# A fused four-layer network on one core: other orders and semaphores in the router stage, the layer-0 feed-forward and the 16-head attention

## The reference

```python
x = x + tanh(g_xattn[0]) * L0_xattn(layernorm(x), ctx, ...)      # attention, one head
x = x + tanh(g_ffn[0])   * L0_ffn(layernorm(x), W_up, W_down, W_gate, W_expert)
x = x + tanh(g_xattn[1]) * L1_xattn(...)                         # 32 heads, rotary
x = x + tanh(g_ffn[1])   * L1_ffn(...)                           # ternary weights
x = x + tanh(g_xattn[2]) * L2_xattn(layernorm(x), ctx, Wq, Wk, Wv, Wo, gq, gk)
x = x + tanh(g_ffn[2])   * L2_ffn(layernorm(x), w_router, wg, wu, wd, ...)
x = x + tanh(g_xattn[3]) * L3_xattn(ctx, layernorm(x), ...)      # scan over 16 states
x = x + tanh(g_ffn[3])   * L3_ffn(layernorm(x), weight)          # fp8 blocks

# L2_xattn: 16 heads of 128; q and k are divided by their root mean square
q = rmsnorm(hidden @ Wq, gq); k = rmsnorm(ctx @ Wk, gk); v = ctx @ Wv
out = softmax(q @ k.T / sqrt(128)) @ v @ Wo

# L2_ffn: 8 routed experts, 2 for each token, beside a shared expert with a gate
probs = softmax(x @ w_router.T); top_v, top_i = top_k(probs, 2)
out = sum over the two of top_v * (silu(x @ wg.T) * (x @ wu.T)) @ wd.T
out += sigmoid(x @ gate_w.T) * (silu(x @ sw_gate.T) * (x @ sw_up.T)) @ sw_down.T
```

## Time and profile before

| what | value |
|---|---|
| runs | 3429.04, 3439.06, 3434.04 us, median 3434.04 |
| profiled execution | 3425.45 us, its span 3423.7 us |
| PE, DVE, ACT, POOL busy | 3077.1, 2608.9, 1870.1, 1471.5 us (90, 76, 55, 43%) |
| layer-0 feed-forward | about 212 to 404 us of the span |
| 16-head attention | about 1400 to 2712 us |
| router stage | about 2712 to 2869 us |

### The profile page before, as it was taken

How to read it: one execution, slowest core, us unless ns; L and a number is a source line. 1 busy time by engine, 2 the same in 40 slices (tenths; PEclk the granted TensorE clock), 3 DMA queues, 4 the chain that set the end, 5 groups by cost and what they waited for, 6 DMA issues and landing times. The chain is left out here.

```text
span 3423.7 us, 43286 instructions
## 1 busy us (share of the span) xinstructions
PE 3077.1 (90%) x14500; PEld 1876.2 (55%) x14500; DVE 2608.9 (76%) x3454; ACT 1870.1 (55%) x3464; POOL 1471.5 (43%) x965
## 2 busy tenths in 40 slices
PE   7969788999997999699999999999998697998985
PEld 3447554333334556465656556655655376786663
DVE  7955688877774999288888888888888764766886
ACT  5654343666664677466666566666666333663220
POOL 1132378000000010177777777778877653224430
PEclk9989999999998999899999999999999898999998
DMA  4147645222214222355565565555554356674321
GB/s 136 50 168 277 231 127 132 67 57 61 60 31 140 74 80 72 141 169 178 194 197 182 169 205 188 182 183 189 179 173 157 106 204 216 248 259 174 141 74 62
DMA packets 228071, 508.06 MB, mean 148 GB/s; under 512 B 36607, under 2 KB 70015, under 8 KB 209936
## 3 DMA queue, kind: packets, MB, share of 16 engines
q1 hardware_dynamic: 221616, 488.55, 43.2%
q0 software_dynamic: 6240, 16.81, 1.4%
HBM read 408.48 MB, written 100.45 MB: 149 GB/s over the span
## 5 line engine op out<-in xcount | busy, mean ns | idle before, releaser
L2473 POOL TENSOR_TENSOR l2x_inflow<-l2x_dtu,l2x_rows_b 128x512 f32<-128x512 f32 x256 | 438.5, 1713 | 217.4 <-DVE l2x_state L2359 211.0
L2489 POOL TENSOR_TENSOR l2x_y_sum<-l2x_y_sum,l2x_state 128x512 f32<-128x512 f32 x224 | 387.2, 1729 | 29.2 <-DVE l2x_state L2368 29.2
L2359 DVE TENSOR_TENSOR_SCAN l2x_state<-l2x_decay,l2x_inflow 128x512 f32<-128x512 f32 x256 | 391.8, 1530 | 0.3 <-issue 0.3
L1358 DVE TENSOR_REDUCE l1x_mx<-psum 128x2 f32<-128x1024 f32 x256 | 308.2, 1218 | 94.0 <-PE psum L1200 92.3
L1315 ACT ACTIVATE l1x_split<-psum 128x1024 f32<-128x1024 f32 x256 | 262.1, 1025 | 154.9 <-PE psum L1200 154.9
L186 POOL TENSOR_TENSOR ln_work<-ln_work,minus_half 128x4 f32<-128x4 f32 (+1 forms) x34 | 36.4, 1071 | 720.0 <-DVE ln_work L170 719.9
L2368 DVE TENSOR_TENSOR l2x_state<-l2x_state,l2x_rows_c 128x512 f32<-128x512 f32 x256 | 315.1, 1231 | 6.6
L2230 ACT ACTIVATE l2x_decay<-l2x_dt,a_neg 128x512 f32<-128x512 f32 x256 | 181.4, 721 | 194.2 <-DVE l2x_state L2359 194.2
L126 PE MATMUL psum<-l2x_probs_t,l2x_v_tok 128*128 128x512 f32 x512 | 234.9, 602 | 13.1 <-ACT l2x_qt L220 10.9
L2166 ACT ACTIVATE l2x_probs<-psum,l2x_soft,l2x_norms 128x512 f32<-128x512 f32 x256 | 195.9, 775 | 87.6 <-DVE l2x_soft L2297 87.6
L126 PE MATMUL psum<-l2x_kt,l2x_qt 128*128 128x512 f32 x512 | 228.7, 593 | 0.9 <-DVE x_res L226 0.9
(11 more groups left out here) (459 smaller groups left out, 7241.6 us busy)
## 6 DMA issues: line engine op xcount, KB each, us to landing
l2x_rows_b<-l3x_xd_dram SPq DMA_DIRECT2D x256, 256.0 KB, 3.9
l2x_rows_c<-l3x_xd_dram SPq DMA_DIRECT2D x256, 256.0 KB, 3.5
l2w_raw<-l_w SPq DMA_DIRECT2D x38, 1024.0 KB, 6.1
l2x_wkv<-l2x_kv_dram SPq DMA_DIRECT2D x32, 1024.0 KB, 6.9
l2x_wq<-l2x_wq_dram SPq DMA_DIRECT2D x16, 2048.0 KB, 7.8
l2w_raw<-l_w SPq DMA_DIRECT2D x38, 512.0 KB, 4.6
l1x_heads_dram<-l1x_stage SPq DMA_DIRECT2D x32, 512.0 KB, 3.3
l2x_wo<-l_wo SPq DMA_DIRECT2D x16, 1024.0 KB, 7.2
```

The costliest lines, as they stand in the source:

```text
L1358: main.drain(dve.tensor_reduce(mx[:, gg % 2, :, j, t], g["psum"][:, b:b + 2, :], AX.X, ALU.max), f"m{n}_0", banks=2)
L2359: dve.tensor_tensor_scan(state[:, s % KEPT, :], decay[:, s % 3, :], inflow[:, s % 3, :], 0.0, ALU.mult, ALU.add).then_inc(scan_done, 1)
L2473: pool.tensor_tensor(inflow[:, s % 3, :], dtu[:], rows_b[:, s % 3, :], ALU.mult).then_inc(inflow_ready, 1)
L2489: pool.tensor_tensor(total, total, state[:, s % KEPT, :], ALU.add).then_inc(added, 1)
```

## The change

- Layer-0 feed-forward: the semaphore `weights_in` is replaced by `router_in` and `expert_in`. PE's wait for both loads is gone. ACT waits for the router before it rounds the router, and for the expert before it rounds the expert. POOL waits for `router_lo` before its first weight.
- 16-head attention, ACT: the square of the fourth query stands ahead of the exponents of the fourth head; its copy stays behind them.
- 16-head attention, DVE: the moments of the next batch stand ahead of `keys_turned`; the normalised rows stay behind it.
- Router stage: PE, ACT, DVE and the order list have the first quarter product between the first two batches; DVE makes the low part of the first weight, between moments and rows; POOL's splits wait until the rows of a batch are written; the last logits come ahead of the up half of `shared_up(2, 0)`, the ranks ahead of `shared_down(1)`, and `place` ahead of DVE's part of it.
- Router stage, scatters: one semaphore for each half of 8 tiles, and the ids are copied and scattered for the second choice half by half.

```diff
@@ l0_ffn
-            for w, name in ((router, "l0_router"), (raw[2], "l0_expert")):
-                sp.dma_start(w[:], ...).then_inc(weights_in, 16)
+            sp.dma_start(router[:], ...).then_inc(router_in, 16)
+            sp.dma_start(raw[2][:], ...).then_inc(expert_in, 16)
@@ tensor
-            pe.wait_ge(weights_in, 32)
@@ scalar
-            act.wait_ge(weights_in, 32)
+            act.wait_ge(router_in, 16)
...
                     weight_round(1)
+                    act.wait_ge(expert_in, 16)
                     weight_round(2)
@@ gpsimd
+            pool.wait_ge(router_lo, 1)
@@ l2_xattn, scalar
                 key_scale(u + 1, 2)
+                query_square(u + 1, 3)
                 exponent(u, 3)
                 decays(u, 8)
-                query(u + 1, 3)
+                query_copy(u + 1, 3)
@@ l2_xattn, vector
                 gather(u, 10)
+                next_norm(u)
                 keys_turned(u + 1)
                 x_turned(u + 2)
-                next_norm(u)
+                next_rows(u)
@@ l2_route, tensor
             route(0)
+            shared_up(0, 0)
             x_turned(1)
             logits_turned(0)
             route(1)
-            shared_up(0, 0)
             shared_up(0, 1)
...
             route(3)
-            shared_up(2, 0)
+            shared_up(2, 0, (("g", 0),))
             logits_turned(3)
+            shared_up(2, 0, (("u", I2),))
             shared_up(2, 1)
+            ranks()
             shared_down(1)
             shared_up(3, 0)
-            ranks()
@@ scalar
             up_split(0)
-            down_split(0)
             act.activation(rows[:, 0:ST, 0:D], g["xn"][:], ACT.Copy).then_inc(rows_copied, 1)
             route(0)
+            down_split(0)
+            shared_silu(0, 0)
             x_turned(1)
...
-            shared_silu(0, 0)
             shared_silu(0, 1)
@@ vector
             x_turned(0)
-            norm(1)
+            ln.moments(dve, 0, 1)
+            up_split(0)
+            ln.apply(dve, 0, 1, rows_of(1))
+            shared_up(0, 0)
...
-            norm(3)
+            ln.moments(dve, 2, 3)
             shared_gate(0, slice(0, ST))
-            shared_up(0, 0)
+            ln.apply(dve, 2, 3, rows_of(3))
...
-            shared_up(2, 0)
             logits_turned(3)
             probabilities()
+            shared_up(2, 0)
             shared_up(2, 1)
+            place()
             shared_down(1)
             weights()
             shared_up(3, 0)
-            place()
@@ gpsimd
-            up_split(0)
+            ln.pool(pool, 0)
+            pool.wait_ge(ln.xn_ready, ST + 1)
             down_split(0)
             ln.pool(pool, 1)
+            pool.wait_ge(ln.xn_ready, 2 * ST + 1)
             up_split(1)
             down_split(1)
             ln.pool(pool, 2)
+            pool.wait_ge(ln.xn_ready, 3 * ST + 1)
             up_split(2)
...
-            scatter(0, 0, NT)
-            pool.wait_ge(scattered[0], NT * 16)
-            pool.tensor_copy(rows[:, :, D].bitcast(I32), tokens[:, 1, :]).then_inc(ids_set, 1)
-            pool.wait_ge(ids_set, 2)
-            scatter(1, 0, NT)
+            scatter(0, 0)
+            scatter(0, 1)
+            for half in range(2):
+                part = slice(half * NT // 2, (half + 1) * NT // 2)
+                pool.wait_ge(scattered[0][half], NT // 2 * 16)
+                pool.tensor_copy(rows[:, part, D].bitcast(I32), tokens[:, 1, part]).then_inc(ids_set, 1)
+                pool.wait_ge(ids_set, 2 + half)
+                scatter(1, half)
```

More of the change, by code:

```diff
@@ L749, in _ @@
         def _(sp):
-            for w, name in ((router, "l0_router"), (raw[2], "l0_expert")):
-                sp.dma_start(w[:], a[name].rearrange("(c p) d -> p c d", p=P)).then_inc(weights_in, 16)
+            sp.dma_start(router[:], a["l0_router"].rearrange("(c p) d -> p c d", p=P)).then_inc(router_in, 16)
+            sp.dma_start(raw[2][:], a["l0_expert"].rearrange("(c p) d -> p c d", p=P)).then_inc(expert_in, 16)
             def piece(m):
@@ L2350, in next_norm, with next_rows @@
                         ring.wait_for(dve, 0, drained=[f"out{G2 - 1}_{t}" for t in range(ST)])
-                    ln.vector(dve, b, (b + 1) % NB, lambda: ring.wait_filled(dve, 0, f"xt{b}_{DC - 1}"))
+                    ln.moments(dve, b, (b + 1) % NB)
+            def next_rows(u):
+                if u % G2 == 1:
+                    b = u // G2
+                    ring.wait_filled(dve, 0, f"xt{b}_{DC - 1}")
+                    ln.apply(dve, b, (b + 1) % NB)
             def scan(u, n):
@@ L2625, in l2_route @@
             "gu_hi", "gu_lo", "dn_hi", "dn_lo", "hid_hi_done", "hid_ready")]
-        gu_in, dn_in, scattered = [[sem(f"{n}{k}") for k in range(2)] for n in ("gu_in", "dn_in", "scattered")]
+        gu_in, dn_in = [[sem(f"{n}{k}") for k in range(2)] for n in ("gu_in", "dn_in")]
+        scattered = [[sem(f"scattered{k}_{half}") for half in range(2)] for k in range(2)]
         ln = LayerNorm(g, sem)
@@ L2682, in _ @@
             for k in range(2):
-                sp.wait_ge(scattered[k], NT * 16)
+                for half in range(2):
+                    sp.wait_ge(scattered[k][half], NT // 2 * 16)
             sp.wait_ge(gu_in[1], (NA // 2 + 1) * 16)
@@ L2709, in logits_turned, with shared_up @@
                 ring.fill(last)
-            def shared_up(n, m):
+            def shared_up(n, m, which=(("g", 0), ("u", I2))):
                 b = n // SHARED
@@ L2716, in shared_up @@
                         pe.wait_ge(xt_back, 16)
-                for x, off in (("g", 0), ("u", I2)):
+                for x, off in which:
                     ring.wait_for(pe, 0, free=f"{x}{n}_{m}")
@@ L3072, in up_split @@
             def up_split(s):
+                pool.wait_ge(gu_lo, s)
                 pool.wait_ge(gu_hi, s + 1)
@@ L3086, in hidden_split, with scatter @@
                                        hidden_hi[:, n % 2, m, :].bitcast(F32), ALU.subtract).then_inc(hid_ready, 1)
-            def scatter(k, first, last):
-                for t in range(first, last):
+            def scatter(k, half):
+                for t in range(half * NT // 2, (half + 1) * NT // 2):
                     pool.indirect_dma_start(g["xs_dram"], bass.IndirectOffsetOnAxis(ap=slot[:, k, t:t + 1], axis=0),
                                             rows[:, t, :], None, bounds_check=SLOTS2 - 1, oob_is_err=False
-                                            ).then_inc(scattered[k], 16)
-            up_split(0)
+                                            ).then_inc(scattered[k][half], 16)
+            ln.pool(pool, 0)
+            pool.wait_ge(ln.xn_ready, ST + 1)
             down_split(0)
             ln.pool(pool, 1)
+            pool.wait_ge(ln.xn_ready, 2 * ST + 1)
             up_split(1)
```

19 lines of the change are left out of this document (12 added, 7 removed).

## The result

The changed kernel takes 3388.27 us (median of 4 runs, 3383.53 to 3391.18) against 3436.55 for the kernel before beside it (4 runs, 3429.04 to 3442.07): ratio 0.986, 95% interval 0.9836 to 0.9883. 3390 was forecast. Its profiled execution took 3387.94 us (span 3386.2, granted clock 0.962 on average); that of before took 3425.45, at 0.963.

The account below looks back on a forecast made before the run. TensorE was busy 1240 of 1312 us in attention, and a chain through slots and scatters ended the router stage. Gains 5.9 + 1.8 + 18.4 + 17.6 = 43.7 us take 3434.0 to 3390, range 3377 to 3408.

Parts of the forecast that it names:

- Layer 0: Layer-0 feed-forward: with router and expert on two semaphores PE starts when the phase opens; net gain 5.9 us, bounds 3 and 6.7.
- For the clock 0.5 us was taken off: Layer 0: an allowance of 0.5 us within the net gain of 5.9; the lower bound 3 allowed for all of the clock.
- 1 us to spare: Layer 0: POOL's split behind the router's small split ends at 221.3, PE asks for it at 222.2.
- The rule weighed in the prediction: Attention moments: two-input DVE and SBUF-reading GpSimd instructions contend, first holding the pair throughout; moments would stand until 1588.6.
- Query's square: Attention, ACT: squaring the last query ahead of the last exponents gains 0.19 us a unit; term 1.8, bounds -4 and +5.
- Moments: Attention, DVE: moments fill the wait for transposed keys; 4.6 us by four long units, 18.4, bounds 8 and 19.5.
- Rival A: Attention: POOL's power blocks the moments until 1588.6; 18.4 becomes about 10, time 3398; chance 0.13.
- Router stage, front: Router stage up to the slots: last logits at 2777 instead of 2788.5, first scatter 2800.2 against 2811.69, 11.5 us.
- Router stage, back: Scatters: wait of 7.43 us goes, ids copy costs about 1; stage ends 18.0 us earlier, 17.6 taken, bounds 6 and 21.
- rival B's second clause: Router stage: landing lag of 7.43 returns at the end as loads and scatters share engines; 9 not 17.6; B's chance 0.16.
- The added waits of POOL for finished rows: Router stage: they keep POOL's splits from starting, at most 1 to 2 us each, with nothing of PE's due.

Follow-up runs that it names:

- e6: The changed kernel without GpSimd's wait for the router's small split in layer 0; 3399.64 us.
- e2: The kernel before with only the last query squared ahead of the last exponents; 3427.85 us.
- e3: The kernel before with only the moments ahead of the keys; 3413.89 us, ratio 0.9935.
- e8: The changed kernel with TensorE's sums of squares waiting for the four squares instead of the last query's copy; 3374.33 us, ratio 0.9834 to the kernel before.
- e11: The changed kernel with the edits of e7 and e8 together; 3370.61 us, ratio 0.9794 to the kernel before.
- e4: The kernel before with only the new orders of the router stage, scatters still awaited as 16 and then 16; 3417.6 us, ratio 0.9944.
- e5: The kernel before with only the scatters in halves on four semaphores, orders as before; 3431.48 us.
- e7: The changed kernel with GpSimd's last three splits ahead of the scatters given to VectorE, behind the slots; 3382.83 us.
- e10: The changed kernel with the four loads of the routed experts' weights issued behind the landing of all scatters; 3410.19 us.
- e9: The changed kernel again, unchanged; 3391.20 us, ratio 0.9859 to the kernel before.
- e12: The kernel before again, unchanged, for a second profile; 3431.55 us, ratio to itself 0.9997.

## Why the prediction was right, point by point

The time fell inside the range, 1.7 us under the likeliest value, and the waits that were named are the waits that went. Lengths of like phases over all profiles are a better measure than the first pair. Kernels with the old and the new form of each phase (layer 0 without e6, the attention without e2, e3, e8 and e11, the router stage without e4, e5, e7, e10 and e11, which have other forms):

| term | forecast | old form, mean | new form, mean | measured |
|---|---|---|---|---|
| layer 0 | 5.9 | 192.1 (6 profiles) | 186.0 (7) | 6.1 |
| attention (square and moments) | 1.8 + 18.4 | 1310.9 (5) | 1292.5 (5) | 18.4 |
| router stage | 17.6 | 156.0 (5) | 138.3 (4) | 17.7 |
| sum | 43.7 | | | 42.2 |

**Layer 0: right.** PE starts 0.38 us after the opening, where 0.15 was forecast. For the clock 0.5 us was taken off, a term that no run shows. What they show is larger on both sides. In the changed kernel it is 4.38 us from the router product to the up product (220.45 to 224.83), 2.78 in the first profile of before: 1.6. But PE ran at half clock for 26 us of this phase in the five other profiles with the old form (16 in the first), against 19 or 20 in the seven with the new one, so the mean gain is 6.1 all the same. POOL's wait for the router's small split was counted as 1 us to spare; e6 shows that it is worth 3.9. The rule weighed in the prediction (the Trainium skill, SBUF — State Buffer, "Who interferes with whom") holds here: of DVE's two-input step and POOL's, whoever is first keeps the pair to its end; in e6 DVE's ends at 222.74, POOL's at 222.69.

**Query's square: right.** 0.19 in a plain unit, 0.15 in a long one; the first unit cost 1.16 (e2) to 1.35 (the changed kernel) instead of 1.0. Over the units of e2 it is 1.8, as forecast.

**Moments: right, a size too good.** 4.6 us was forecast for each of the four long units; alone (e3) it is 4.36, so 17.4 instead of 18.4. The 4.6 of the changed kernel has a part of the square in it, which the forecast counts under its own term. Rival A is refuted by the rows above: a power by POOL does not hold up DVE's small steps, whether with two inputs or with one. By the same section of the Trainium skill the two-input ones would wait; for this operation the trace disagrees, for the splits (e6, and 4.53 and 2.43 us in the changed kernel) it agrees.

**Router stage, front: right.** First scatter 84.3 us into the stage (84.3 to 85.8 in four profiles), 85.0 forecast. But it is the sum that held: the logits were 12.3 us earlier, not 11, and the slot steps, with POOL's three splits on top, lost 8.6 us (e7 has them without). At most 2.9 us of the first scatter's time was lost by that: POOL's own splits ended only at 2778.05, and the scatter stood 2.85 us behind them. A part of the gain that the prediction only touches on is the clock: from 14 to 26 us into the stage PE had a granted clock of 0.50 in the first profile of before (2729 to 2742), during and behind the idle time of 8.28 us, and 1.00 in the changed kernel (2710 to 2723), where the quarter product fills it.

**Router stage, back: right in the first profile, a size too good in most.** From the first scatter to the next load 50.7 was forecast. It was 51.0 in the first profile, and 54.6, 52.9, 55.3 and 53.9 in e5, e6, e8 and e9, against 56.7 to 59.3 in six profiles with one wait. The mean gain is about 4, not 6.5. The term that was mis-sized is the scatters': "with two halves ... 7.43 goes, and a second copy of the ids comes in, about 1". The pause between the halves did shrink by 7.2 us on average. But it had been time in which the DMA engines worked off what had queued (their share is 0.93 in the 8 us from 2834 of the first profile of before), and 1.5 us of it came back behind the last scatter, as rival B's second clause says. And the second sixteen scatters, copy included, take 22.9 us instead of 20.6: in three of the five profiles one of them starts inside a subtraction by DVE that before fell among the first sixteen or into the pause (2.93 us instead of 0.97, last section).

That the total of the stage still measures 17.7 is in part luck. It rests on e12's one long stage; without it the old form's mean is 154.8, and the gain 16.5.

**A step that was wrong**, though on the good side: "The added waits of POOL for finished rows keep its splits from starting, at most 1 to 2 us each, with nothing of PE's due." I priced them as costs only. They forbid the order of events that e12 shows, in which a split by POOL catches DVE's rows. In the old form DVE's first rows always take 8.12 us, the second ones 1.92 in five profiles and 8.30 in one; in the eight profiles with the new orders all of them take 1.91 or 1.92.

**The gap of 48 against 37.5.** The first profile of before was good in layer 0 (by 3) and in the router stage (by 2 against the mean of its likes, 7 against e12). In the two phases of layer 1, which nothing touches, it took 2.7 us less than the changed kernel's. Like phases give 42.2, inside the interval of 40 to 56 us for the medians' difference. The runs of before spread over 23 us (3423.8 to 3447.0), with medians from 3429.0 to 3439.9 us on four chips; those of the changed kernel, which are far fewer (8), over 9 (3383.5 to 3392.9). The slow ones of before have the lower granted clock: 0.963 in the run of 3423.8, 0.953 in that of 3447.0. Where the other 6 us and e4's large ratio come from stays open. e12's order of events is at most a part of it, and only one profile caught it. That profile is 21.5 us longer than the first of before, of which 7.3 lie in the router stage, 3.1 in layer 0 and 8.7 in layer 1 (1008.0 us against 999.3, and 998.5 to 1004.6 in the twelve others), and what stretches layer 1 no run explains.

## What to carry to other kernels

Read how an operation may be caught by another engine's long one, and let the long one wait for the short one's semaphore; in layer 0 such a wait cost POOL 0.5 us (its split starts 2.5 us after the opening, 2.0 in e6) and was worth 3.9. In the router stage it forbids an order of events that the first profile doesn't show and that made the stage 5 to 7 us longer (e12). When a producer's last step is moved, look at what its consumer awaits: moving the square gave 0.19 us a unit, awaiting it instead of the copy gave 1.03 more. A wait for DMA that is split in two gives back only what isn't the engines' own backlog; look at their busy share in that stretch first.

## What the runs showed of the hardware that was not expected

- A power by POOL (128x16, 2.92 us) holds up none of DVE's steps; a subtraction by POOL (128x2048, 4.5 to 4.7 us) held up steps of 0.16 to 0.3 us to its end, and DVE's four rows of 1.92 us in all through two of its operations, to 8.12 and 8.30.
- The other way about, a scatter by POOL takes 0.97 us to issue, but those that start inside a subtraction by DVE of 2048 columns took 2.3 to 3.0, in every profile, and end 0.84 to 0.88 us behind the subtraction (timelines of DVE and POOL of the changed kernel):

```profile
2803.74 2.29 DVE L3009 TENSOR_TENSOR l2w_w_lo<-l2w_raw,l2w_w_hi 128x2048 fp32r<-128x2048 f32 x1 [1.26 <-issue]
2803.96 2.93 POOL L3113 DMA_INDIRECT l2f_xs_dram<-l2f_rows,l2f_slot  x1 [0.79 <-POOL l2f_rows L3143]
```

- The same 2560 scatter packets took 22 us of all 16 engines' time without other loads. Beside 3.1 MB of loads they took 23.6 to 27.2 with a pause between the two sixteens, and 23.3 to 33.1 without one, where nothing that I found sets the best profile apart.
